# Cross-attention, projection and self-attention in one program, on a drawn SBUF map

## The reference

```python
x = x + xattn(layernorm(x), ctx, Wq, bq, Wkv, bkv, Wproj, bproj)   # 16 heads of 32, softmax over 1601 rows
x = x + attn(layernorm(x), WQ, WK, WV_down, WV_up)                 # 16 heads of 64
x = x + ffn(layernorm(x), Wg, bg, W1, b1, W2, b2)                  # 8 experts, top 2

# xattn:
out = softmax((q * SCALE) @ k.T) @ v          # for each batch and head
return out @ Wproj + bproj
# attn: scores are K Q^T / 8 with an upper triangle mask; only the diagonal of the
# softmax is used:
v_down = diag(softmax(scores)) * (x @ WV_down)
return x + mean over heads of v_down @ WV_up
```

## Time and profile before

| | |
|---|---|
| runs | 1511.16 us median of 3 (1510.75 to 1514.27) |
| the profiled execution's own time | 1517.16 us |
| its span | 1515.3 us |
| TensorE matmuls busy | 1335.7 us, 88% of the span |
| VectorE busy | 948.8 us, 63% |
| ScalarE busy | 763.0 us, 50% |
| GpSimd busy | 91.3 us, 6% |

### The profile page before, as it was taken

The page is one execution under the profiler, slowest core; times in us unless marked ns, Lnnn a source line. Parts: engine busy times, 40 slices in busy tenths (PEclk is TensorE's granted clock), DMA queues, the critical chain, the costliest instruction groups (busy, mean ns, idle before and its releaser), DMA issues. The chain is left out here.

```text
span 1515.3 us, 21885 instructions
## 1 busy us (share of the span) xinstructions
PE 1335.7 (88%) x7363; PEld 1158.1 (76%) x7364; DVE 948.8 (63%) x1485; ACT 763.0 (50%) x1322; POOL 91.3 (6%) x60
## 2 busy tenths in 40 slices
PE   5999999999999999999999998404999459999995
PEld 4888888888888888888888887303887347877774
DVE  4666666666666666666666665417578646287882
ACT  3455555555555555555555554302432336477771
POOL 0000000000000000000000000023622110000002
PEclk9999999999999999999999999756999779999998
DMA  5210110110111011020011000095252475399992
GB/s 180 77 60 29 32 56 28 31 56 28 29 58 28 27 60 28 25 62 28 24 53 37 24 15 8 21 234 93 56 188 91 156 260 191 101 348 310 350 311 96
DMA packets 129458, 147.18 MB, mean 97 GB/s; under 512 B 66296, under 2 KB 66680, under 8 KB 129408
## 3 DMA queue, kind: packets, MB, share of 16 engines
q1 hardware_dynamic: 128144, 142.54, 30.4%
q0 software_dynamic: 1280, 4.20, 0.8%
HBM read 126.06 MB, written 20.64 MB: 97 GB/s over the span
## 5 line engine op out<-in xcount | busy, mean ns | idle before, releaser
L497 DVE SCALAR_TENSOR_TENSOR Ks<-ps_scores,bkc,Ks 64x384 fp32r<-64x384 f32 (+2 forms) x254 | 160.6, 632 | 147.3 <-ACT Ks L381 144.6
L147 PE MATMUL ps_scores<-cT_hi,Wkv_hi 128*128 128x384 f32 (+2 forms) x508 | 184.4, 363 | 6.4 <-DVE Wkv_lo L519 6.4
L148 PE MATMUL ps_scores<-cT_lo,Wkv_hi 128*128 128x384 f32 (+2 forms) x508 | 175.6, 346 | 0.0
L149 PE MATMUL ps_scores<-cT_hi,Wkv_lo 128*128 128x384 f32 (+2 forms) x508 | 175.5, 345 | 0.0
L459 ACT ACTIVATE Pr<-ps_scores,stat 128x705 f32<-128x705 f32 (+1 forms) x128 | 119.6, 934 | 108.1 <-DVE stat L587 108.1
L147 PE MATMUL ps_scores<-Wkv_hi,cT_hi 128*128 128x512 f32 (+1 forms) x412 | 171.3, 416 | 0.4 <-DVE Ks L497 0.4
L381 ACT ACTIVATE Ks<-ps_scores,bkc 64x384 fp32r<-64x384 f32 (+2 forms) x254 | 149.3, 588 | 42.8 <-PE ps_scores L149 40.9
L446 ACT CAST PT<-ps_turn 128x512 fp32r<-128x512 f32 (+2 forms) x256 | 110.3, 483 | 116.2 <-PE ps_turn L747 115.4
L503 DVE TENSOR_TENSOR Vs<-ps_scores,Vs 128x512 fp32r<-128x512 f32 (+1 forms) x103 | 71.2, 691 | 153.9 <-ACT Vs L385 152.9
L148 PE MATMUL ps_scores<-Wkv_lo,cT_hi 128*128 128x512 f32 (+1 forms) x412 | 162.8, 395 | 0.0
L149 PE MATMUL ps_scores<-Wkv_hi,cT_lo 128*128 128x512 f32 (+1 forms) x412 | 162.8, 395 | 0.0
(11 more groups left out here) (311 smaller groups left out, 2478.9 us busy)
## 6 DMA issues: line engine op xcount, KB each, us to landing
wu_raw<-in_L_ffn_W_dram SPq DMA_DIRECT2D x64, 1024.0 KB, 7.3
raw<-in_ctx_dram SPq DMA_DIRECT2D x16, 768.0 KB, 4.5
raw<-in_ctx_dram SPq DMA_DIRECT2D x8, 1024.0 KB, 5.2
raw<-in_ctx_dram SPq DMA_DIRECT2D x8, 512.0 KB
o_heads<-U SPq DMA_DIRECT2D x64, 64.0 KB, 1.8
oA<-o_heads SPq DMA_DIRECT2D x8, 512.0 KB, 16.3
sorted_x<-zeros SPq DMA_DIRECT2D x1, 4096.0 KB, 15.0
sorted_out<-zeros SPq DMA_DIRECT2D x1, 4096.0 KB, 24.7
```

Of the source, the lines that this page charges most:

```text
L147: nc.tensor.matmul(out_ap, sh, mh, start=(i == 0), stop=False)
L148: nc.tensor.matmul(out_ap, sh, ml, start=False, stop=False)
L149: last = nc.tensor.matmul(out_ap, sl, mh, start=False, stop=(i == len(pairs) - 1))
L497: ins = nc.vector.scalar_tensor_tensor(out=Ks[c][64:128, j, o:o + wide], in0=acc[64 * h:64 * h + 64, 0:wide], scalar=bkc[:, j:j + 1], in1= ...
```

## The change: what it does

Programs 1 and 2 become one. Each tile gets a fixed address: an area `EARLY` to `LATE` and one from `LATE` to `END`. While batch 7 is worked on, tiles of program 1 that are no longer read give their place to the tiles of the joining, the projection and the first weights of the heads.

- The outputs of batches 0 to 6 (448 tokens, `OLD`) come back from DRAM during unit (7, 0), and their factors are worked out there as well (`vector_factors`, `scalar_factors`, `tensor_factors`).
- Batch 7's outputs don't go to DRAM: `U` is moved into `o7` by 8 small SBUF-to-SBUF transfers for each chunk, and its factors are spread over the partitions by two matmuls with a 0/1 matrix (`spread7`, `X7`).
- The sums, scalings and joins of batches 0 to 6 all stand on GpSimd (`pool_seam`), and start when unit (7, 0) is over.
- In the steps of unit (7, 1) a function `beside(i)` of each engine inserts the rest: on ScalarE and VectorE the split of `Wproj` after step 3, the split of `oT` after steps 4 and 5, the residual and bias after step 6, batch 7's first factors after step 7; on ScalarE the cast of the first two weights of the heads after steps 6 and 8; on TensorE half a tile of the projection in each of steps 6, 7 and 8.
- After unit (7, 1) come the rest of the projection, batch 7's joining, the last tile's projection (it holds batch 7), and the layer norm in two parts: three tiles, then the last one.
- The weights 2 and 3 of the heads are loaded after the projection, since their slots lie where `Wproj` and `oT` lie.

```diff
-        with nc.Block() as block:
+        def program(block):
@@ unit of each engine, last batch
-                unit(B - 1, 0, turns_before(B - 1, 0), KC)
-                unit(B - 1, 1, turns_before(B - 1, 0) + LAST_TURNS, 0)
+                unit(BE, 0, turns_before(BE, 0), KC, beside=lambda i: vector_factors(dve, i))
+                unit(BE, 1, turns_before(BE, 0) + LAST_TURNS, 0, beside=lambda i: vector_beside(dve, i))
+                vector_seam(dve)
+                vector_heads(dve)
@@ SyncE
+        def sync_seam(sp):
...
+            sp.wait_ge(sem("u_free"), 128 * BE + 1)
+            sp.wait_ge(sem("turned"), turns_before(BE, 0) + turn_of_ctx(KC - 1) + 1)
+            load_old_outputs(1)
+            sp.wait_ge(sem("kv_made"), KV_LAST + KC + SUBS[1][0][1])
+            load_old_outputs(0)
+            sp.wait_ge(sem("f_turned"), 1)
...
+            sp.wait_ge(sem("o_summed"), PAIRS_0 + NP + 1)
+            sp.wait_ge(sem("kv_made"), KV_LAST + PIECES[1])
+            move_new_outputs(0)
+            sp.wait_ge(sem("r_out"), 32)
...
+                        sp.dma_start(oR[r0:r0 + HD, c, :, :], src.partition_broadcast(HD)).then_inc(sem("oR_in"), 16)
...
+            sp.dma_start(Wp_raw[:, :, :], Wproj.rearrange("(k p) n -> p k n", p=P)).then_inc(sem("wp_in"), 16)
+            sp.dma_start(x_sum[:, :, :], x_rows).then_inc(sem("x_again"), 16)
+            sp.wait_ge(sem("oA_in0"), 64)
...
+            load_head_weights(sp, 0)
+            load_head_weights(sp, 1)
+            sp.wait_ge(sem("o_summed"), PAIRS_1 + NP + 1)
+            move_new_outputs(1)
@@ ScalarE
+        def scalar_beside(act, i):
+            if i == 3:
+                act.wait_ge(sem("wp_in"), 16)
+                nc.scalar.copy(Wp_hi[:, :, :], Wp_raw[:, :, :]).then_inc(sem("wp_hi"), 1)
+            elif i in (4, 5):
+                scalar_old_hi(act, 2 * (i - 4))
+                scalar_old_hi(act, 2 * (i - 4) + 1)
+            elif i == 6:
+                head_weights_hi(act, 0)
+            elif i == 7:
+                act.wait_ge(sem("shifted7"), 1)
+                nc.scalar.activation(part7[:, :, :], part7[:, :, :], ACT.Exp).then_inc(sem("exp7"), 1)
+            elif i == 8:
+                head_weights_hi(act, 1)
@@ TensorE
+        def tensor_beside(pe, i):
+            if i == 6:
+                pe.wait_ge(sem("wp_lo"), 1)
+                project(pe, 0, (0, 1))
+            elif i == 7:
+                project(pe, 0, (2, 3))
+            elif i == 8:
+                project(pe, 1, (0, 1))
```

More of the change, by code:

```diff
@@ new lines, in tensor_heads, with take, slot_ready, columns @@
+        def tensor_heads(pe):
+            def take(use):
+                before = use_before(use)
+                if before is not None:
+                    pe.wait_ge(sem("b_done"), before + 1)
+                return use_bank(use)
+            def slot_ready(w):
+                pe.wait_ge(sem("sw_lo"), w + 1)
+                return w % SLOTS2
+            def columns(kind, half, use0):
+                at = slot_ready(UNITS2.index((kind, half)))
+                for j in range(HP):
+                    cols = slice(j * P, (j + 1) * P)
+                    three(pe, take(use0 + j), [((W2_hi[at][:, k, cols], W2_lo[at][:, k, cols]),
+                                                (x2T_hi[:, k, :], x2T_lo[:, k, :])) for k in range(KC)]) \
+                        .then_inc(sem("b_made"), 1)
+            def values(half):
+                at = slot_ready(UNITS2.index(("V", half)))
@@ new lines, in score_bank @@
+            def score_bank(half, i):
+                n, w = i // 2, i % 2
+                j, h = n // 2, n % 2
+                if i % 4 == 0:
+                    pe.wait_ge(sem("b_done"), USE_K[half] + j + 1)
+                out_bank = take(s_use(half, i))
+                window = slice(2 * w * P, 2 * (w + 1) * P)
+                for r in range(2):
+                    g = 2 * w + r
+                    keys = slice(g * P, (g + 1) * P)
+                    ins = three(pe, out_bank[:, 2 * P * r:2 * P * (r + 1)],
+                                [((KT_hi[:, j, h, keys], KT_lo[:, j, h, keys]),
+                                  (QT_hi[:, j, window], QT_lo[:, j, window]))])
+                ins.then_inc(sem("b_made"), 1)
@@ L1294, in perceiver_kernel @@
+            for t in range(TT - 1):
+                up(0, t)
+            turn_values(1)
+            up(0, TT - 1)
+            for t in range(TT):
+                up(1, t)
+        with nc.Block() as block:
+            program(block)
         NE, _, H = W1.shape
```

1330 lines of the change are left out of this document (711 added, 619 removed).

## The result

The changed kernel takes 1458.49 us (median of 4, 1458.34 to 1459.3); the kernel before took 1512.72 (4 runs, 1510.75 to 1514.5). The ratio is 0.9640, 95% interval 0.9629 to 0.9652: 54.2 us less, where 40 were forecast.

The account below looks back on a forecast made before the run. It took TensorE's 54.5 us hole, behind transfers and a GpSimd and VectorE chain, as what could be gained. With 54.5 and 4.4 gained, 19 paid: 1511.2 - 40 = 1471, taken as 1472 us; 8 in 10 from 1459 to 1487.

Parts of the forecast that it names:

- The hole: From 975.1 to 1029.6 us TensorE does next to nothing; the forecast has all 54.5 us of it gone.
- Slower: Rival, chance 0.03: new tile addresses up to unit (7, 0) cost access time; at 4.5% the gain is gone.
- a loop over batches of another length: Sign that the forecast is wrong: the loop over batches 0 to 6 changes in duration.
- the seam: From the end of unit (7, 1) to the heads' first query matmul: forecast at 27 us.
- step 6: In unit (7, 1), residual and bias sum plus projection: +6.7 us, 3.5 of it waiting beside GpSimd's weight split.
- step 3: In unit (7, 1), loading and splitting Wproj delays the softmax: +5.9 us, bounds 2.6 and 10.
- Steps 4 and 5: In unit (7, 1), low parts of oT, GpSimd's work and TensorE's half clock: +3.4 and +2.0 us.
- Steps 7 and 8: In unit (7, 1), two small VectorE instructions and ScalarE's exponential ahead of the last transposes: +0.9 us.
- so I add 3.5: Last tile's norm after unit (7, 1): 3.5 us added to 2.75 for tensor-scalars slowed beside the zeroing of the keys.
- All is covered: Rival, chance 0.15: Wproj lands by 954, VectorE precedes each split, clock holds; unit +9, seam 24, total 1458 us.
- No change: Rival, chance 0.02: TensorE's wait for oT_lo merely moves into the unit, if oR lands only after 985.
- the starved softmax: Rival, chance 0.18: later Wproj, full GpSimd waits and half clock leave 22 us less instead of 40, 1489 us.

Follow-up runs that it names:

- split1_late: The changed kernel with GpSimd's second weight split held back until both products of batch 7's factors with the diagonal are made; 1466.02 us.
- after_pad_ct: The changed kernel with an unused tile of 32 bytes between Vs0 and cT, so cT starts at 0 within 64 bytes; ratio 0.9671 to the kernel before.
- wide_ts: The changed kernel with two small tensor-scalars of the last tile's norm working on the columns of all four tiles; 1461.57 us.

## Why the prediction was right and wrong

- **The hole.** Right: 54.5 us of hole went, the work behind it moved into unit (7, 1) and paid there. Unit (7, 0) took its instructions for nothing (53.9 us from its start to its last `U`, as before within 0.2).
- **"Nothing of it touches the loop over batches 0 to 6."** This step failed: it was put at nothing without a reason and measured -4.9 us up to the end of unit (7, 0). The drawn map alone gives 5.1 us less in the time (interval -7.1 to -3.3) and 4.6 in the trace. I had the mechanism as the rival "Slower", as a loss only; that addresses could also make it faster was not among the cases, though "a loop over batches of another length" stood among the signs of being wrong. The time missed the range by only 0.5 us, so that this step, the seam or step 6 put right by itself would have brought it inside; step 3 erred the other way.
- **Step 3, +5.9 us.** Mis-sized: +9.7, counted to the `U` of step 4 (+9.3 to its maximum). `Wp_raw` landed 20.0 us after the unit's start instead of 18.4, `Wp_lo` took 3.17 us instead of 2.28 plus 0.6, and without the change the step would have come 1.6 us earlier than in the first profile, since TensorE's clock was back sooner (0.89 instead of 0.70 over steps 1 to 3). That `Wproj` bounds the step was half true: with it on time the unit is only 2 us shorter, and the waits for `oR`'s products take over.
- **Steps 4 and 5, +3.4 and +2.0.** +2.5 and +1.4; half clock as described (the outputs took 1.65 us instead of 0.98).
- **Step 6, +6.7.** Mis-sized: +1.6. The wait of 3.5 us did not come, as VectorE was ready 0.11 us before GpSimd; in `split1_late` and `after_pad_ct` it did. Of the other 3.2 us half did not come either; that the instruction filled gaps in which VectorE had waited is a guess. The forecast was right for one side of a race that I took to be decided.
- **Steps 7 and 8, +0.9.** +0.8.
- **The seam, 27 us.** 22.0. Up to the factors' product with the diagonal the forecast holds (T+6.1 against T+6.2, the lock of 4.29 us included), and up to the low part of the last tile it is 0.9 us long (T+10.5 against T+11.4). The mis-sized term is "so I add 3.5" for tensor-scalars beside the zeroing: the norm of the last tile took 3.25 us, not 6.25. `wide_ts` shows the condition that I had left out, several elements in a row. The terms of the last part add up to T+23.5 and T+26.4, where I wrote T+23.7 and rounded to T+27; that slip is 0.6 us of the 5.0.
- **Heads and program 3.** +1.9 and -1.9 us against the second profile of before; the heads are 123.7 us, as forecast against the first. Not tested further: the same program 3 took 330.8 and 326.9 us in the two executions of the kernel before.
- **The rivals.** "All is covered" gives the measured time, 1458, but by luck and not for its reasons: its unit of +9 and its early `Wproj` did not occur. "No change" and the starved softmax did not either.
